# Homes of the first sets, GpSimd's queue and the end of the biases in a kernel of four conditioned layers

## The reference

```python
x = x + conv1d(x, w0, 9 taps, 4 groups) + (cond @ c_w0.T + fside)[:, :, None]
x = x + einsum('boi,bih->boh', agg_w1, x) + agg_b1[:, :, None]
x = x + conv1d(x, w2, 9 taps, 4 groups) + (cond @ c_w2.T + fside)[:, :, None]
x = x + einsum('boi,bih->boh', agg_w3, x) + agg_b3[:, :, None]
# agg_w[b] = sum over 8 experts of att[b, k] * weight[k], agg_b = att @ bias_k
# att = softmax of a small network of cond, one for each sample
```

## Time and profile before

| | us |
|---|---|
| runs of the kernel, median of 3 (lowest to highest) | 2476.83 (2476.41 to 2477.38) |
| the profiled execution's own time | 2478.66 |
| its span | 2476.9 |
| TensorE busy | 2456.8 |
| VectorE busy | 2117.9 |
| ScalarE busy | 1514.4 |
| GpSimd busy | 19.7 |

### The profile page before, as it was taken

The page is one execution under the profiler, slowest core; times in us unless marked ns, Lnnn a source line. Parts: engine busy times, 40 slices in busy tenths (PEclk is TensorE's granted clock), DMA queues, the critical chain, the costliest instruction groups (busy, mean ns, idle before and its releaser), DMA issues.

```text
span 2476.9 us, 99072 instructions
## 1 busy us (share of the span) xinstructions
PE 2456.8 (99%) x45256; PEld 1478.0 (60%) x45256; DVE 2117.9 (86%) x813; ACT 1514.4 (61%) x1118; POOL 19.7 (1%) x25
## 2 busy tenths in 40 slices
PE   8999999999999999999999999999999999999998
PEld 3444444555555555566666666666666666666665
DVE  7988988988988889889889888898898898888984
ACT  5666666666666666666666666666666666666655
POOL 3000000000000000000000000000000000000000
PEclk9999999999999999999999999999999999999999
DMA  9644444444444444444444454444444444444433
GB/s 334 215 135 127 147 149 127 131 154 138 127 136 157 131 127 152 144 127 137 152 135 127 142 153 128 127 157 139 127 142 151 131 127 147 150 127 128 159 104 121
DMA packets 186683, 357.24 MB, mean 144 GB/s; under 512 B 12754, under 2 KB 143834, under 8 KB 154010
## 3 DMA queue, kind: packets, MB, share of 16 engines
q1 hardware_dynamic: 186056, 354.60, 45.7%
q10 hardware_dynamic: 594, 2.13, 0.3%
HBM read 205.69 MB, written 150.99 MB: 144 GB/s over the span
## 4 chain that ended last, share of the span: by engine, by line
PE 97%; DMA 2%; DVE 1%; issue 1%; ACT 0%; SPq 0%; DVEq 0%; ACTq 0%
PE psum L412 61%; PE psum L483 35%; DMA xin<-x 1%; DVE diff L763 1%; DMA mix_dram<-shared 1%; PE psum L388 0%; PE psum L361 0%; PE psum L339 0%; ACT shared L637 0%; DVE y L802 0%; SPq L178 0%; DVE outb L873 0%; DVE shared L802 0%; PE psum L344 0%; SPq L172 0%
## 5 line engine op out<-in xcount | busy, mean ns | idle before, releaser
L412 PE MATMUL psum<-diff,prod_w 32*64 32x512 f32 x28672 | 1691.1, 588 | 7.0 <-ACT shared L653 3.5
L412 PEld LDWEIGHTS psum<-diff,prod_w 32*64 32x64 f32 x28672 | 961.7, 131 | 632.6 <-issue 323.7
L763 DVE TENSOR_TENSOR diff<-xin 128x2052 f32<-128x2052 f32 x256 | 976.9, 3909 | 310.7 <-PE psum L412 306.7
L483 PE MATMUL psum<-y,mixw 32*64 32x512 f32 x16384 | 1026.7, 587 | 0.4 <-ACT bias_table L699 0.4
L483 PEld LDWEIGHTS psum<-y,mixw 32*64 32x64 f32 x16384 | 579.1, 131 | 336.7 <-issue 166.7
L763 DVE TENSOR_TENSOR diff<-x 128x2055 f32<-128x2055 f32 x255 | 569.1, 2307 | 0.0
L729 ACT ACTIVATE x<-psum,bias_now 128x2048 f32<-128x2048 f32 x128 | 251.7, 1967 | 196.0 <-PE psum L483 196.0
L684 ACT ACTIVATE outb<-psum,bias_now 128x2048 f32<-128x2048 f32 x128 | 251.2, 1962 | 195.1 <-PE psum L483 195.1
L653 ACT COPY shared<-psum 128x2048 f32<-128x2048 f32 x128 | 238.9, 1867 | 175.5 <-PE psum L412 168.5
L850 DVE TENSOR_TENSOR y<-y,shared 128x2048 f32<-128x2048 f32 x126 | 289.6, 2298 | 15.9 <-ACT y L669 15.9
L677 ACT COPY y<-psum 128x2048 f32<-128x2048 f32 x126 | 235.7, 1871 | 91.8 <-PE psum L412 91.8
(11 more groups left out here) (83 smaller groups left out, 101.9 us busy)
## 6 DMA issues: line engine op xcount, KB each, us to landing
xin<-x SPq DMA_DIRECT2D x128, 1024.0 KB, 6.9
out<-outb SPq DMA_DIRECT2D x127, 1024.0 KB, 4.8
mixw<-mix_dram SPq DMA_DIRECT2D x512, 128.0 KB, 5.3
mix_dram<-shared SPq DMA_DIRECT2D x6, 1024.0 KB, 13.9
mix_dram<-y SPq DMA_DIRECT2D x6, 1024.0 KB, 11.9
mix_dram<-diff SPq DMA_DIRECT2D x2, 1024.0 KB, 12.4
mix_dram<-outb SPq DMA_DIRECT2D x2, 1024.0 KB, 13.3
y<-experts ACTq DMA_DIRECT2D x2, 512.0 KB, 4.4
```

The lines of the kernel that those rows point to most:

```text
L412: return pe.matmul(psum[cols, half, g, :], prod_w[v][at, kind, s, cols], moving, start=start, stop=stop, skip_group_check=True)
L483: mm = pe.matmul(psum[cols, half, r, :], mixw[home][at, b, g, cols], y[home][at, :, g, b, :], start=g == 0, stop=g == GROUPS - 1)
L763: nc.vector.tensor_tensor(into(kind), in0, in1, op).then_inc(diff_ready[v], 1)
```

## The change

Two more homes are added, both in `x2`, and sets 6 and 7 live there, so `shared[0]` holds no set. The second x and the matrices of `mix(0, 0)` are issued by GpSimd, after its work on the taps, with semaphores of their own, x first. SP's queue issues the stores one after another; its wait for stores 0 to 7 moves into its first step. GpSimd no longer clears all of x2 at the start; it clears only the gaps, behind its loads. `finish_biases` runs inside the first mixing, behind its first four matmuls, writes into B_HALF, and waits for set 15 to be copied out; ScalarE copies set 15 ahead of the biases.

```diff
-                 outb[:, 0, :], outb[:, 1, :]]
+                 outb[:, 0, :], outb[:, 1, :], x2[:, 0:PH * BANK], x2[:, PH * BANK:2 * PH * BANK]]
-        home_of = [0, 1, 4, 5, 2, 3, 6, 7, 8, 9, 0, 1, 4, 5, 10, 11]
-        LAST_IN_SHARED, LAST_IN_Y, LAST_IN_DIFF = ((6, 7), (10, 11)), ((4, 5), (12, 13)), (8, 9)
+        home_of = [0, 1, 4, 5, 2, 3, 12, 13, 8, 9, 0, 1, 4, 5, 10, 11]
+        LAST_IN_SHARED, LAST_IN_Y, LAST_IN_DIFF, LAST_IN_X2 = (10, 11), ((4, 5), (12, 13)), (8, 9), (6, 7)
...
+        def x_there(n):
+            if whole(n) and n == 1:
+                return second_x_loaded, 16 * PB
+            return x_loaded, 16 * PB * (1 if whole(n) and n == 0 else n)
+
+        def mix_there(m, n):
+            if m == 0 and whole(n) and n == 0:
+                return first_mix_loaded, MIX_LOADS
+            return mix_loaded[m], MIX_LOADS * (n + m)
...
             load_taps(1)
-            for j in range(SETS // 2, SETS):
-                store_agg(j)
-            sp.wait_ge(taps_ready[0], 1)
-            for j in range(SETS):
-                sp.wait_ge(agg_stored[j], 16)
-            load_mix_on(sp, 0, 0)
-            sp.wait_ge(diff_ready[0], PRODUCTS)
-            load_x_on(sp, 1)
-            for j in range(SETS, AHEAD):
+            for j in range(SETS // 2, AHEAD):
                 store_agg(j)
 
             def step(i):
                 if whole(i) and i == 0:
                     for j in range(AHEAD, 2 * SETS):
                         store_agg(j)
+                    for j in range(SETS):
+                        sp.wait_ge(agg_stored[j], 16)
...
-            pool.memset(x2[:], 0.0).then_inc(x2_clear, 1)
...
+            pool.wait_ge(diff_ready[0], PRODUCTS)
+            load_x_on(pool, 1, second_x_loaded)
+            pool.wait_ge(taps_ready[0], 1)
+            for j in range(SETS):
+                pool.wait_ge(agg_stored[j], 16)
+            load_mix_on(pool, 0, 0, landed=first_mix_loaded)
+            halves = x2[:].rearrange("p (j c) -> p j c", j=PAR)
+            pool.memset(halves[:, :, 0:PH * T].rearrange("p j (k w) -> p j k w", w=ROW)[:, :, :, R:ROW], 0.0)
+            pool.memset(halves[:, :, PH * T:HALF], 0.0).then_inc(x2_clear, 1)
...
-                into = psum[:, A, m, 0:B]
+                into = psum[:, B_HALF, 2 * m, 0:B]
...
+            def finish_biases():
+                pe.wait_ge(*taken(AHEAD + 1))
+                for m in range(2):
+                    finish_bias(m)
...
-                    mix(0, 0, (agg_part, 1), taken(AHEAD), taken(AHEAD + 1), nothing, parts=True)
+                    mix(0, 0, (agg_part, 1), taken(AHEAD), (bias_ready, 2), finish_biases, parts=True)
...
-                    pe.wait_ge(agg_part, 1)
-                    for m in range(2):
-                        finish_bias(m)
-                    pe.wait_ge(bias_ready, 2)
...
-                else:
-                    act.wait_ge(agg_stored[LAST_IN_SHARED[v][0]], 16)
+                elif v == 1:
+                    act.wait_ge(agg_stored[LAST_IN_SHARED[0]], 16)
...
                     take_agg(AHEAD)
+                    take_agg(AHEAD + 1)
                     for m in range(2):
                         act.wait_ge(bias_pe, m + 1)
-                        nc.scalar.copy(bias_table[:, LEAD * PB:LEAD * PB + B, m], psum[:, A, m, 0:B]
+                        nc.scalar.copy(bias_table[:, LEAD * PB:LEAD * PB + B, m], psum[:, B_HALF, 2 * m, 0:B]
                                        ).then_inc(bias_ready, 1)
-                    take_agg(AHEAD + 1)
```

More of the change, by code:

```diff
@@ L134, in conditioned_layers @@
         x_loaded = sem("x_loaded")
+        second_x_loaded = sem("second_x_loaded")
+        first_mix_loaded = sem("first_mix_loaded")
         diff_ready = [sem(f"diff_ready{v}") for v in range(2)]
@@ L168, in same_home_before, with load_x_on, load_mix_on @@
             return max(k for k in range(j) if home_of[k] == home_of[j])
-        def load_x_on(queue, n):
+        def load_x_on(queue, n, landed=x_loaded):
             for b in range(PB):
-                queue.dma_start(xin[:, b * XROW + PH:b * XROW + PH + L], x[PB * n + b]).then_inc(x_loaded, 16)
-        def load_mix_on(queue, m, n, home=None):
+                queue.dma_start(xin[:, b * XROW + PH:b * XROW + PH + L], x[PB * n + b]).then_inc(landed, 16)
+        def x_there(n):
[6 more added lines that the diff above has]
+            return mix_loaded[m], MIX_LOADS * (n + m)
+        def load_mix_on(queue, m, n, home=None, landed=None):
             home = m if home is None else home
+            landed = mix_loaded[home] if landed is None else landed
             src = mix_dram[m].rearrange("b (g i o) -> i b g o", g=GROUPS, i=CG)
@@ L178, in load_mix_on @@
                 queue.dma_start(mixw[home][CG * r:CG * (r + 1)], src[:, bass.ds(PB * n, PB)]
-                                ).then_inc(mix_loaded[home], 16)
+                                ).then_inc(landed, 16)
         def whole(i):
@@ L492, in mix @@
                     pe.wait_ge(y_ready[m], 2 * n + 2)
-                pe.wait_ge(mix_loaded[m], MIX_LOADS * (n + 1))
+                pe.wait_ge(*mix_there(m, n))
                 pe.wait_ge(*a_free)
@@ L555, in last_two @@
                 pe.wait_ge(y_ready[1], 2 * n + 3)
-                pe.wait_ge(mix_loaded[0], MIX_LOADS * (PAIRS + 1))
+                pe.wait_ge(mix_loaded[0], MIX_LOADS * PAIRS)
                 half_mix(0, 0, lambda: half_mix_tail(1, 1), lambda: pe.wait_ge(y_ready[1], 2 * n + 4))
@@ L654, in take_sums @@
                 into = y[home][:].rearrange("p j g b m -> p j g (b m)")
-                if whole(n) and n == 0:
-                    act.wait_ge(agg_stored[LAST_IN_SHARED[v][1]], 16)
+                if whole(n) and n == 0 and v == 1:
+                    act.wait_ge(agg_stored[LAST_IN_SHARED[1]], 16)
                 act.wait_ge(conv_done[v], done + 3)
@@ L743, in diff_of_xin @@
             def diff_of_xin(n, kinds):
-                dve.wait_ge(x_loaded, 16 * PB * (n + 1))
+                dve.wait_ge(*x_there(n))
                 eighths = xin[:].rearrange("p (m c) -> p m c", c=BLOCK)
```

## The result

The kernel became slower. Ten runs of each gave a median of 2484.64 us against 2478.30, a ratio of 1.0025 with a 95% interval of 1.0015 to 1.0035: 6 us, above the 5 us (0.2%) that the forecast called the least that can be told. It is also above the top of its range, 2480.5, even less the 1.5 us by which the kernel before was slower here than in the runs of the forecast (2478.30 and 2476.83). One of the ten runs of the changed kernel took 3901.82 us at a granted clock of 0.625 and is left out of the ratio. The profiled span went from 2476.9 to 2482.8.

The account below looks back on a forecast made before the run. TensorE, busy 99% of the span, was taken as the bound, with recoverable losses before 100 us. Gain 57.24 - (T + 3.65) + 0.96 + 0.27, 1.4 us off the 2476.83 median, gave 2475.4; range 2472.0 to 2480.5.

Parts of the forecast that it names:

- the hole shrinks, 3.07 + 1.48 us: TensorE's 3.54 us idle at 40.12 us falls to about 0.4: 3.07 gained, plus 1.48 from the clock not falling.
- I take 51: Second x issued by GpSimd at 40.5: its second half lands at 51 us, within bounds 47.8 to 54.9.
- The bound of 54.9: Latest landing forecast for the second x's second half, 13.51 us after issue, as behind a full backlog.
- the new queue need not stand behind the backlog: GpSimd's loads need not wait for SP's issued stores, as DMA engines take turns between queues packet by packet.
- T = 53.4: T is when the first mixing's matrices land: 8.7 us after the middle issue at 44.7, bounds 48.6 to 59.2.
- I charge the 1.48 again: Before the first mixing, TensorE idles 3.1 us from 50.25; a clock loss of 1.48 us is charged, bound 0.
- 1.5 us for the move: Moving the six bias matmuls inside the first mixing costs 1.5 us of the 4.55 gained, leaving 3.0.
- The waits at 97 us vanish: VectorE's earlier start removes TensorE's 0.96 us wait at 96.94 and the 0.27 us in the convolution behind it.
- The sum: Total gain over the kernel before, 54.8 less the matrices' landing time: 1.4 us, at most 4.2.
- Rival C: First mixing's matrices land late, at 56 to 60 us, taking turns with SP's stores: 2478 to 2482; chance 0.18.
- B: The forecast itself: waiting for matrices replaces waiting for the store, landing 52.2 to 56: 2473.5 to 2478; chance 0.45.
- Rival D: Issuing DMAs from GpSimd is itself slow, so the matrices land after 60 us: 2482 to 2490; chance 0.07.

Follow-up runs that it names:

- homes only: The changed kernel keeping only sets 6 and 7 in x2 and the small clears, with SP's queue order and biases as before; ratio 0.9995 to the kernel before.

## Why the prediction was wrong, point by point

- *Sets 6 and 7 in x2: the hole shrinks, 3.07 + 1.48 us.* Right. Set 15 began 4.56 us earlier (4.55 forecast), with the clock at full speed.
- *x(1) through GpSimd's queue: "I take 51".* Wrong: 55.2. The bound of 54.9 was nearly right, the choice inside it not. The step that failed is that the new queue starts at once and shares. It stood 4.6 us, while 1.9 MB of stores already issued went first. ScalarE's queue stood 3.6 us, a GpSimd queue used before 4.9, and with the stores held x moved after 1.5 us.
- *The Trainium skill's rule in "DMA: Bandwidth & Descriptors"* (engines take turns between queues, section on queues, rings and completion order): the trace agrees to the packet while both queues move (211 and 212; 641 and 643). The conclusion put behind it, that the new queue need not stand behind the backlog, is half borne out: 918 packets of SP's queue went first, and as many that had been issued before x did not.
- *mix(0,0): "T = 53.4".* This term is one of the two that failed: 57.56, 4.16 too late. In the run with held stores it is 53.27. Of the 4.3 us between these two, 3.2 are the later start of x (45.38 against 42.22) and 1.1 the slower way from x's first packet to the mixing (12.2 us beside the stores, 11.0 without them). That 53.27 is so near to the forecast is luck, for there no store shared the engines, as the forecast had it.
- *"I charge the 1.48 again".* The second term that failed. The clock's price was taken from a pause whose lower clock fell on 3 us of work; here it lay on 8 us of work, and the run with nine filling matmuls measures 3.78. The runs don't show that it goes by the length of the pause; they show less with the biases ahead (1.69 and 3.06) than inside (3.23 to 4.97).
- *The biases: 1.5 us for the move, their 2.18 us behind T.* Right in kind. Its price at full clock is 2.29 when the matrices are late. What the forecast lacked is that moving them also takes work out of the pause, which then grows from 5.3 to 7.4 us.
- *The waits at 97 us vanish.* Right, but here partly because TensorE itself came 6 us later; with TensorE early and x late they grew (2.83 us in "homes only"), and with x first on SP's queue they were gone.
- *The sum.* Forecast 1.4 us gained; less 4.16 for T and 2.30 for the clock gives 5.1 lost, and the trace has 4.82 at 121.81. Rival C was what happened: its mechanism (in turn with SP's stores) and T between 56 and 60, with a chance of 0.18. Its rule, which should read slower by T - 54.8, gave 2.8 us, since it carried the same 1.48. Two bounds were summed wrongly: C up to T = 59.5 ends at 2481.5 by that rule, not at 2480.5, and B's lower end, T = 52.2, at 2474.2, not at 2473.5. The measured time lies beyond either.
- *Rival D and the rule of "SBUF — State Buffer"* in the Trainium skill (descriptors from GpSimd held up by VectorE): no sign of it. Two issues of x took 1.32 us and four of the matrices 2.37, and with the same work on VectorE beside it x moved after 1.5 us once the stores were held.
- *Not forecast:* the rest of the difference in the runs. The ratio says 6.2 us, the trace 4.82 up to the end of the loop. There TensorE has two pauses with no releaser, 0.80 and 0.37 us before, and after:

```profile
2373.41 7.74 PE L428 MATMUL psum<-diff,prod_w 32*64 32x512 f32 x127 [1.10 <-issue]
...
2382.38 3.69 PE L428 MATMUL psum<-diff,prod_w 32*64 32x512 f32 x61 [1.24 <-issue]
```

That is 1.17 us more, and closes the span. Over the thirteen traces the sum of these pauses is 0.56 to 2.85 us with no relation to the edits that I can see (2.45 and 2.50 with filling, 0.64 with the queue used before). Whether it belongs to a build or to an execution was not tried, so about one of the 6 us isn't settled.

## What to carry to other kernels

A load moved to a second queue doesn't pass bulk transfers that were issued before it on the first; here 1.4 to 1.9 MB of them went first. Issue the urgent load ahead of the bulk transfers: this was fastest with both on SP's queue, x first, then the matrices, then the stores. When a wait moves, work that used to lie beside it is worth keeping there; a pause on TensorE can cost its length and then the lower clock on what follows, here 3.8 us for a pause of 7.4 and 3.2 for one of 1.4. And a hole closed on one chain is a gain only if the other chain that meets it is early too: the homes alone gained 4 us at the mixing and kept 1.5.

## What the runs showed of the hardware that was not expected

Stores issued on one queue went ahead of a later load on another at 0.41 MB/us: for 4.6 to 5.0 us (1.9 MB) when the second queue was GpSimd's, in five traces, and for 3.6 us (1.4 MB) when it was ScalarE's, in one. Other stores that had also been issued before the load, some 2 MB, moved beside it or after it. Rows of 512 bytes went in packets of 4 KB from GpSimd's queue and of 512 bytes from ScalarE's; beside 2 KB packets that gave 54% and 26% of the engines. With seven filling matmuls the clock fell at 59.4 us with TensorE at work again for 1.7 us, after a pause of 1.36 us that followed 6.3 us of dense matmuls, and came back at 66.3; with the pause closed it did not fall.
